# Four graph layers over 50,000 nodes: the softmax chains of three passes and the preparation rewritten

## The reference

```python
x = _layernorm(x + _L0_gnn_ref(x, edge_attr_64, edge_index, ...))   # q, k, v, 16 heads, edges gated by tanh
x = _layernorm(x + _L1_gnn_ref(x, edge_index, ...))                 # GAT, 4 heads, with self loops
x = _layernorm(x + _L2_gnn_ref(x, edge_index, ...))                 # two GATv2 layers (8 heads; 1 head), then a product
x = _layernorm(x + _L3_gnn_ref(x, edge_index, edge_attr_64, ...))   # 4 heads, denominator over all edges
```

```python
e = jax.nn.leaky_relu(xl[src] + xr[dst], NEG_SLOPE)
logits = jnp.einsum('ehc,hc->eh', e, att)
ex = jnp.exp(logits - m[dst])
alpha = ex / denom[dst]
out = jax.ops.segment_sum(xl[src] * alpha[..., None], dst, num_segments=N)
```

## Time and profile before

| | us |
|---|---|
| median of 3 runs | 4066.97 |
| the runs | 4057.2 to 4076.98 |
| the profiled execution, whole | 4061.93 |
| its span, first to last instruction | 4060.2 |

### The profile page before, as it was taken

The page is one execution under the profiler, slowest core; times in us unless marked ns, Lnnn a source line. Parts: engine busy times, 40 slices in busy tenths (PEclk is TensorE's granted clock), DMA queues, the critical chain, the costliest instruction groups (busy, mean ns, idle before and its releaser), DMA issues. The chain is left out here.

```text
span 4060.2 us, 72393 instructions
## 1 busy us (share of the span) xinstructions
PE 3500.2 (86%) x19961; PEld 2510.3 (62%) x20169; DVE 3558.8 (88%) x6756; ACT 2879.2 (71%) x9715; POOL 2308.0 (57%) x2305
## 2 busy tenths in 40 slices
PE   2999999999987999986999969999867777687775
PEld 2888888888864777764666645555534444354443
DVE  3899999999986999976999959999979999698786
ACT  2999999999975888875988855555546766344343
POOL 1577777777766777754433323345153442687777
PEclk9999999999988999998999989999989999898888
DMA  1455555555544343324544425555345554454442
GB/s 49 129 149 152 151 152 150 152 152 150 152 140 110 103 105 100 102 61 121 129 126 125 119 75 134 139 137 136 95 127 146 143 147 127 129 133 119 114 117 67
DMA packets 719120, 503.45 MB, mean 124 GB/s; under 512 B 141745, under 2 KB 621335, under 8 KB 718960
## 3 DMA queue, kind: packets, MB, share of 16 engines
q1 hardware_dynamic: 533072, 362.39, 33.0%
q0 software_dynamic: 56528, 81.64, 7.6%
q10 hardware_dynamic: 129360, 57.82, 5.1%
HBM read 304.28 MB, written 200.10 MB: 124 GB/s over the span
## 5 line engine op out<-in xcount | busy, mean ns | idle before, releaser
L1169 POOL DMA_INDIRECT slot_src_rows<-x,src_table_cols x392 | 420.7, 1073 | 453.1 <-PE psum L226 227.4
L237 ACT ACTIVATE node_z<-psum 128x128 f32<-128x128 f32 x1568 | 419.8, 325 | 22.5 <-PE psum L217 14.7
L1169 POOL DMA_INDIRECT slot2a_src_rows<-x,src_table_cols x196 | 220.5, 1125 | 335.0 <-PE psum L226 201.3
L646 ACT ACT_TABLE_LOAD x306 | 392.6, 1283 | 12.9 <-issue 7.7
L237 ACT ACTIVATION_READ_ACCUMULATOR node_z<-psum 128x1 f32 x1568 | 348.5, 227 | 0.0
L237 ACT ACTIVATE slot_logit<-psum 128x128 f32<-128x128 f32 x980 | 256.8, 279 | 125.9 <-PE psum L1337 99.8
L1169 POOL DMA_INDIRECT slot2b_src_rows<-xl,src_table_cols x196 | 198.2, 1011 | 257.1 <-PE psum L226 210.5
L1194 POOL DMA_INDIRECT out_nodes<-slot_new,out_index x196 | 243.0, 1240 | 59.8 <-issue 58.9
L1001 POOL DMA_INDIRECT node_gathered<-in_x,src_cols x196 | 235.8, 1203 | 47.0 <-issue 47.0
L1173 POOL DMA_INDIRECT slot_dst_rows<-in_x,dst_gather_cols x196 | 211.0, 1076 | 84.4 <-issue 50.9
L1166 POOL DMA_INDIRECT map_cols<-slot_map,src_cols x196 | 213.6, 1090 | 59.7 <-issue 59.7
(11 more groups left out here) (417 smaller groups left out, 12180.5 us busy)
## 6 DMA issues: line engine op xcount, KB each, us to landing
x<-node_x SPq DMA_DIRECT2D x294, 256.0 KB, 2.9
slot_neg<-neg SPq DMA_DIRECT2D x147, 256.0 KB, 4.5
node_xT<-in_x_T SPq DMA_DIRECT2D x98, 256.0 KB, 3.1
out_nodes<-node_x SPq DMA_DIRECT2D x98, 256.0 KB, 2.8
x<-slot_new ACTq DMA_DIRECT2D x98, 256.0 KB, 2.3
slot_keep<-keep SPq DMA_DIRECT2D x98, 256.0 KB, 4.2
slot_dst_rows<-x SPq DMA_DIRECT2D x98, 256.0 KB, 5.4
xl<-node_xl SPq DMA_DIRECT2D x98, 128.0 KB, 2.9
```

The source lines that it names most:

```text
L237: ins = act.activation(g.z[u][:, t, :], rows[:, t, :], ACT.Square, scale=float(D ** -0.5), accum_out=sums[u][:, t:t + 1])
L646: act.add_instruction(mybir.InstLoadActFuncSet(name=nc.get_next_instruction_name(), ins=[], outs=[], act_func_set_id=wanted[0]))
L1169: pool.indirect_dma_start(src_rows[u][:, t, 0:src_width], None, table, column(c.src_table_cols[order], u, i, t))\
```

## The change

**Pass "2a".** `v` comes first: PE puts Wl1 src into bank A, ACT copies it with the value's bias into a new tile `val`, then PE adds Wr1 dst onto the same bank (`z`). ACT's `z` is a relu, DVE's `z` is gone. `r` is four products of 512 columns: `src_linear`, `own_linear`, `src_relu`, `own_relu`. The maximum is subtracted by PE, which adds minus the identity times `fmax` onto the logit bank (`e_p`), and ACT reads it from there (`exp_p`); the other exponential is an instruction of its own (`exp`). `o` goes to bank B. The way back over rows is gone: DVE adds `den` and the own edge's exponential (`tot`), ACT takes the logarithm (`ln`) and the exponential of minus that (`inv`), and DVE multiplies (`agg`).

**Pass "0"**: `ln`, `inv`, `agg` take the place of `tot`, `rec`, `rs`, `rB`, `agg`. **Pass "2b"**: DVE's `z` and `e_p` go; ACT makes a relu and a copy (`z`, `zl`), `r` is two products, `e_p`, `exp_p`, `exp` as in "2a".

**Lookups.** Pass "0" has three lookup places to a chunk, and does 116 of the 196 lookups; pass "1" does the other 80, two after each chunk's gathers. They are made in mirrored order, and `source_columns` stands after pass "1".

**Preparation.** The loads are 60, in three groups with a semaphore each (`rows`, `first`, `late`); SP issues 33 and ACT 27. `first_row` begins as soon as the rows are there. The biases are columns: their three levels are made for [128, 5] tiles, turned once by PE, and stand as 15 partitions of one tile.

**Order.** The lists of `PLAN` for "0", "2a", "2b" and "3" are new; those of "1" have two places more. The node pass keeps its list.

```diff
-        "2a": [("DVE", "dst"), ("PE", "z"), ("PE", "zo"), ("ACT", "z"), ("ACT", "zo"), ("DVE", "z"),
-               ("PE", "r"), ("PE", "v")],
-        "2b": [("DVE", "dst"), ("PE", "z"), ("ACT", "z"), ("DVE", "z"), ("PE", "r")],
+        "2a": [("PE", "v"), ("ACT", "v"), ("DVE", "dst"), ("PE", "z"), ("PE", "zo"), ("ACT", "z"), ("ACT", "zo"),
+               ("PE", "r"), ("PE", "o")],
+        "2b": [("DVE", "dst"), ("PE", "z"), ("ACT", "z"), ("ACT", "zl"), ("PE", "r")],
...
+    if layer in ("2a", "2b"):
+        softmax = [("DVE", "fc"), ("DVE", "f"), ("PE", "e_p"), ("DVE", "shift"), ("DVE", "e_c"), ("ACT", "exp_p"), ("ACT", "exp")]
     if layer == "0":
-        sums = [("DVE", "v"), ("DVE", "den"), ("DVE", "pv"), ("PE", "tot"), ("DVE", "num"), ("DVE", "tot")]
+        sums = [("DVE", "v"), ("DVE", "den"), ("DVE", "pv"), ("ACT", "ln"), ("DVE", "num"), ("ACT", "inv"), ("DVE", "agg")]
...
-        sums = [("ACT", "exps"), ("PE", "o"), ("DVE", "den"), ("DVE", "pv"), ("PE", "tot"), ("DVE", "num"), ("DVE", "sv"), ("DVE", "ns")]
+        sums = [("ACT", "exps"), ("DVE", "den"), ("DVE", "pv"), ("DVE", "num"), ("DVE", "sv"), ("DVE", "tot"), ("ACT", "ln"),
+                ("DVE", "ns"), ("ACT", "inv"), ("DVE", "agg")]
...
+    if layer in ("0", "2a"):
+        mean = []
...
     if layer == "0":
-        side += [("POOL", f"dst_gather{t}") for t in range(TILES)]
+        side = [("POOL", f"gather{t}") for t in range(3)] + [("POOL", f"dst_gather{t}") for t in range(TILES)]
+    elif layer == "1":
+        side += [("POOL", "gather_row0"), ("POOL", "gather_row1")]
...
+                elif step == "v" and layer == "2a":
+                    pe.wait_ge(*g.DVE.done(u, i, "dst"))
+                    pe.matmul(A(u), c.Wl1[:, :], src, start=True, stop=True).then_inc(g.pe_out[u], 1)
                 elif step == "z" and layer == "2a":
...
+                    pe.wait_ge(*g.ACT.done(u, i, "v"))
+                    pe.matmul(A(u), c.Wr1[:, :], dst, start=False, stop=True, skip_group_check=True).then_inc(g.pe_out[u], 1)
...
+                    pe.wait_ge(*g.ACT.done(u, i, "z"))
+                    pe.matmul(A(u), c.src_linear[:, :], src, start=True, stop=False)
+                    pe.matmul(A(u), c.own_linear[:, :], dst, start=False, stop=False)
+                    pe.matmul(A(u), c.src_relu[:, :], first, start=False, stop=False)
                     pe.wait_ge(*g.ACT.done(u, i, "zo"))
...
+                    pe.matmul(A(u), c.own_relu[:, :], second, start=False, stop=True).then_inc(g.pe_out[u], 1)
...
+                elif step == "e_p":
+                    pe.wait_ge(*g.DVE.done(u, i, "f"))
+                    pe.matmul((A if layer == "2a" else B)(u), c.minus_ident[:, :], fmax[u][:, 1:CHUNK + 1], start=False, stop=True,
+                              skip_group_check=True).then_inc(g.pe_out[u], 1)
...
                 elif step == "r":
...
+                    pe.matmul(B(u), c.pair_relu[:, :], first, start=True, stop=False)
+                    pe.wait_ge(*g.ACT.done(u, i, "zl"))
+                    pe.matmul(B(u), c.pair_linear[:, :], second, start=False, stop=True).then_inc(g.pe_out[u], 1)
...
+    by_sp = loads["rows"] + loads["first"][0::2] + loads["late"][0::2]
+    by_act = loads["first"][1::2] + loads["late"][1::2]
...
+            v.wait_ge(arrived["rows"], everything["rows"])
...
+            v.wait_ge(arrived["first"], everything["first"])
...
+            v.wait_ge(arrived["late"], everything["late"])
```

More of the change, by code:

```diff
@@ L288, in sb, with fetch, load, column @@
         return ctx.enter_context(nc.sbuf_tensor(name, shape, dt))
-    loads = []
-    def load(name, shape, src, dt=F32, room=None):
+    loads = {"rows": [], "first": [], "late": []}
+    def fetch(into, src, group):
+        loads[group].append((into, src))
+    def load(name, shape, src, dt=F32, room=None, group="late"):
         t = (room or sb)(name, shape, dt)
-        loads.append((t[:], src))
+        fetch(t[:], src, group)
         return t
-    def column(name, src, m=P):
-        return load(name, [m, 1], src.rearrange("(p o) -> p o", o=1))
-    def row(name, src, m=P):
-        return load(name, [P, m], src.partition_broadcast(P))
+    def column(name, src, m=P, group="late"):
+        return load(name, [m, 1], src.rearrange("(p o) -> p o", o=1), group=group)
     own = ExitStack()
@@ L474, in _ @@
             v.wait_ge(masks, 2)
+            v.scalar_tensor_tensor(out=first_row[:, :], in0=keep[0][:, :], scalar=1.0, in1=slot_row[:, :], op0=ALU.subtract,
+                                   op1=ALU.mult).then_inc(firsts, 1)
             for o in range(2):
                 v.tensor_scalar(neg[o][:, :], keep[o][:, :], BIG, -BIG, ALU.mult, ALU.add).then_inc(masks, 1)
[L477 to L479 removed]
@@ new lines, in _ @@
+            v.wait_ge(worked, n)
+            for k in range(len(to_center)):
+                n = did(v.bn_aggr(mean[:, k, :], stats[:, k, :]))
+            v.wait_ge(worked, bias1_at)
+            did(v.tensor_scalar(c.value_bias1[:, :], c.node_bias1[:, :], 1.0, None, ALU.add))
+            v.wait_ge(sums_ready, 1)
+            did(v.tensor_copy(biases[:, 0:3], psum[:, 6, D:D + 3]))
+            did(v.tensor_copy(biases[:, 3:4], wide_bl2[:, :]))
+            biases_at = did(v.tensor_tensor(biases[:, 4:5], wide_bl2[:, :], psum[:, 6, 0:1], ALU.subtract))
@@ new lines, in _ @@
+            marks["src_float"] = count[0]
+            flags_at = [did(v.tensor_tensor(c.last[o][:, :], here[o][:, :], after[o][:, :], ALU.not_equal)) for o in range(2)][0]
+            v.wait_ge(levels_ready, 1)
+            did(v.tensor_copy(tiles_of(c.bias_levels[:, :]), psum[0:LEVELS, 6, 2 * D:3 * D].unsqueeze(1).broadcast_to([LEVELS, TILES, D])))
+            v.wait_ge(worked, n)
+            did(v.tensor_scalar(c.own_relu[:, :], c.S1[:, :], SLOPE - 1.0, None, ALU.mult))
+            did(v.tensor_scalar(c.src_relu[:, :], c.S1[:, :], 1.0 - SLOPE, None, ALU.mult))
@@ L622, in _ @@
-            ins.then_inc(products, 1)
+            pe.wait_ge(made, marks["ident"])
             pe.wait_ge(firsts, 2)
@@ L1208, in _ @@
             if layer == "0":
-                pool.wait_ge(map_ready, SLOT_TILES * 16)
+                pool.wait_ge(map_ready, len(MAP_FIRST) * 16)
+            if layer == "1":
+                for u in g.streams:
+                    pool.wait_ge(looked_up[u], lookups[u] * 16)
             if layer == "3":
@@ L1250, in work @@
                     act_copy(act, g, u, t1[u][:, :], A(u), scale=SLOPE)
+                elif step == "exp_p":
+                    act.wait_ge(*g.PE.done(u, i, "e_p"))
+                    act_copy(act, g, u, expo[u][:, 0, :], (A if layer == "2a" else B)(u), ACT.Exp)
+                elif step == "exp" and layer in ("2a", "2b"):
+                    act.wait_ge(*g.DVE.done(u, i, "e_c"))
+                    act_copy(act, g, u, expo[u][:, 1, :], expo[u][:, 1, :], ACT.Exp)
                 elif step == "exp":
@@ L1638, in work @@
                     ins = v.tensor_tensor(small[u][:, :, :], sums(u), small[u][:, :, :], ALU.add)
+                elif step == "tot" and layer == "2a":
+                    after("den")
+                    after("sv")
+                    ins = v.tensor_tensor(expo[u][:, 2, :], den[u][:, :], expo[u][:, 2, :], ALU.add)
                 elif step == "tot":
@@ L1647, in work @@
                     ins = v.reciprocal(recip[u][:, :, :], small[u][:, :, :])
+                elif step == "agg" and layer in ("0", "2a"):
+                    after("ns" if own else "num")
+                    v.wait_ge(*g.ACT.done(u, i, "inv"))
+                    ins = v.tensor_tensor(agg[u][:, :], (t2 if own else num)[u][:, :], expo[u][:, 2, :], ALU.mult)
                 elif step == "agg":
```

521 lines of the change are left out of this document (277 added, 244 removed), and 38 rows, old and new, of the table PLAN.

## The result

The changed kernel takes 4042.7 us, median of 4 runs (4040.91 to 4043.81), beside 4067.98 (4057.20 to 4076.98) of the kernel before on the same chip: a ratio of 0.9938, 95% interval 0.9917 to 0.9959. It is faster, by 25 us where 147 were forecast, and lies outside the range of 3880 to 3990. The profiled execution took 4040.91 us, its span is 4039.2.

A forecast was written before the change was run, and what follows sets the result against it. Each pass was taken to be bound by its fullest engine's work, not by a chunk's chain. 4060.2 - 37 - 29 - 32 - 46 = 3916, stated as 3920, own range 3890 to 3955, whole range 3880 to 3990.

The forecast's parts named there:

- The node pass, put at 0: Node pass: no other work, since the products that add a bias keep 512 columns; it stays at 1163.7 us.
- Preparation, -37: Preparation: fewer loads for SP to issue and DVE work partly before the last group lands, 37 us less; bounds -20, -42.
- Pass "0", -29: Pass "0": PE loses eight transposes per chunk, 11.40 to 10.8 us per chunk, -29 us; bounds -43 (PE alone) and 0.
- Pass "1", 0: Pass "1": POOL's added lookups fit and DVE, the bound, is untouched: 0 us; bounds -3 and +8.
- Pass "2a", -32: Pass "2a": DVE's work falls and PE becomes the bound, 9.75 us per chunk, -32 us; bounds -37 and -15.
- The joins are paid for: Rival: passes "2a" and "2b" gain nothing, since PE waits for ACT inside a chunk; 3996 us, chance 0.12.
- half of it lost where PE waits for ACT's `v`: Pass "2a", the bound of -15 us: PE waits for ACT's `v` and `z` within one bank.
- slower: Rival: the in-place bank exposes three hand-offs of 1.5 us per chunk in "2a" and "2b"; 4138 us, chance 0.05.
- Pass "2b", -46: Pass "2b": DVE loses `z` and `e_p`, PE gains two products, 8.97 us per chunk, -46 us; bounds -58 and -25.
- Pass "3", 0: Pass "3": POOL is the bound and its gathers and scatters keep their order: 0 us; bounds -8 and +8.
- The clock: Rival: pass "0", now with gaps, falls to a granted clock of 0.9, +15 instead of -29; 3964 us, chance 0.03.
- Two SBUF inputs: Rival: added DVE instructions with two SBUF inputs wait for POOL in "2a" and "0", +40 at most; 3957 us, chance 0.04.

The follow-up runs named there:

- e1: The changed kernel with the bias product's two operands on 128 partitions, the added rows zeros: 3892.24 us, ratio 0.9569 to the kernel before.
- e3: The changed kernel with the bias product's two operands on 65 partitions: 3896.13 us.
- e4: The kernel before, with the product that adds a bias contracting over only the first 32 rows: 4211.74 us, ratio 1.0358.

## Why the prediction was wrong

- **The node pass, put at 0: +105.6. The step that failed.** "The diff gives the node pass no other work: the products that add a bias keep their 512 columns. So 1163.7 stays." Columns were counted and rows were not. 15 rows between products of 128 cost 0.256 us a time, 392 times in the node pass and 588 in all: 150 us, shown by e1, e3 and e4 in both kernels. Without that the change is 3892.2 us, inside the forecast's own range of 3890 to 3955. No rival named it, and the rule of the Trainium skill cited above, which speaks against this edit if a product of few rows counts as a change of mode, was not weighed.
- **Preparation, -37: -39.9.** Right, by its own steps: VectorE waits for the last group until 19.70 us (19.8 forecast) and is done 8.0 us later (8 forecast). The 2.5 us added for hand-offs with PE did not come, so the node pass starts at 28.2 where 29 to 34 was said.
- **Pass "0", -29: -13.1.** The mechanism was right: with 128 rows it is 563.5 us, that is -38.2, between the forecast and PE's bound of -43. Two bias products per chunk took 25.1 of it back. With 128 rows the scan `f` comes every 10.67 us (10.5 to 11.1 forecast), and from 1260 to 1720 us PE is busy for 454.9 of 460 and ACT idle for 44 (82 of 452 before), about half, as was said.
- **Pass "1", 0: +7.9.** The one bias product of a chunk again; 562.9 in e1_rows128 and thus 0.
- **Pass "2a", -32: +1.1.** Two causes, each shown by itself: 13.1 us for the rows and 22.7 for the two stores ahead of ScalarE's copy. With both gone it is -34.7, PE and DVE full, and the scan `f` comes every 9.66 us for 9.75 forecast. The second is the rival *The joins are paid for* in one pass, and its mark was named: "their old time with idle time on PE". The forecast gave "half of it lost where PE waits for ACT's `v`" as its bound and lost two thirds. It had not counted what ScalarE itself does ahead of `v`. The *slower* rival, three hand-offs exposed in each chunk, was far off: one was, for 0.46 us.
- **Pass "2b", -46: -36.7.** The size was a little off: 9.17 us per chunk for 8.97, within its bounds of -58 and -25. The middle of the pass shows which term was too small:

```profile
3060.00:3440.00 380.00, 366.95 (x1567) 213.34 (x1566) 370.84 (x579) 312.00 (x907) 160.27 (x164) 1.00 0.58 158
```

DVE is busy 370.84 of 380 us, 8.95 per chunk of 9.17, where 8.7 stood in the sum: without `z` and `e_p` it does 0.95 us less than its 9.90 before, not 1.20. The chunk is 0.20 longer than forecast, and 49 x 0.20 is the 10 us that are missing. No run took this apart.
- **Pass "3", 0: -45.9.** POOL as the bound was right, and so was the order of its transfers. The step that failed is silent in the text: that a transfer's duration is a constant, so that the same transfers in the same order take the same time. They lasted 1.18 us on average and then 1.06, because VectorE's order moved against them. This error went the other way and hid a third of the first.
- **The clock.** Pass "0" was granted 0.97 as before, so this rival did not occur; in "3" the clock rose from 0.87 to 0.92, as PE's idle time shrank.
- **Two SBUF inputs.** The prediction said "the trace does not bear it out here", having looked at VectorE's durations only. The Trainium skill, page "SBUF — State Buffer", section "Who interferes with whom", has the rule that a DVE instruction with two SBUF inputs contends with a GpSimd instruction that reads SBUF, and that "Issue order, not op shape, decides who blocks". The runs agree with the first, and with the second in one direction only. A transfer that starts second is held: one of 0.97 us takes up to 1.93 before and 2.01 after. A VectorE instruction that starts second is not: of 43 scans `f` between 3520 and 4000 us of the kernel before, 28 began inside a running transfer and took 1.28 us like the other 15. So here POOL alone pays, and the rival had put the price on DVE. (Its sum was too large besides: with the slacks that it names, 0.15 and 0.7 us per chunk, 26 us are left and not 40.) The earlier trace rows had held the sign, a mean of 1087 ns for transfers whose shortest in that window is 0.94.

## What to carry to other kernels

Before an operand is made small to save space or loads, look at what TensorE runs on either side: a product of at most 64 rows among products of 128 cost a quarter of a microsecond, as much again as the product itself, and padding with zeros to 65 took it all back. Put what an in-order engine must do for another (the copy into which an in-place sum waits) ahead of its own DMA issues. Where an engine with indirect transfers is the bound, read the spread of their durations against what VectorE does at their start before calling its time fixed; here half a microsecond more of VectorE work, rightly placed, took 5% off a pass.
